# New places in the engines' queues for a fused attention and mixture-of-experts block

## The chip, the cores and the metric
The kernel runs on one core of one Trainium2 chip. The metric is the device time of one execution in microseconds (us). Before the change three runs took 1023.67, 1023.90 and 1024.99 us; the median is 1023.9. All arithmetic is float32. PE is the matmul engine (TensorE), DVE is VectorE, ACT is ScalarE, POOL is GpSimd and SP is SyncE, which here only issues DMAs.

## The reference, cut to what matters
```
xn  = layernorm(x)                                  # x: 4 x 1024 tokens x 128
# attention: 16 query heads, 8 key/value heads of 64, rotary embedding, gate per head
q, k, v, gate = split(xn @ w_attn);  q, k = rope(q), rope(k)
G   = cumsum(log_sigmoid(6.9 + gate))               # over time
a   = exp(2 log|q k / 8| + G_t - G_s - max),  causal
y   = layernorm_per_head(a @ v / (sum(a) + 1e-6)) * ln_w
attn = y @ w_proj
# experts: 7 routed (top 2, capacity 366) and one shared
h   = layernorm(xn) * ln_g + ln_b
idx, gates = top2 softmax(h @ Wr);  pos = place of the token in its expert
routed = gates * ((silu(xe @ W1) * (xe @ W3)) @ W2)  # scattered to the experts and back
shared = (silu(h @ W1s) * (h @ W3s)) @ W2s
out = x + attn + routed + shared
```

## The kernel before
The 4096 tokens are four chunks (the batch rows) of 1024, each eight blocks of 128. The kernel has a setup and then 32 pairs (p = 0 to 31: chunk p // 8, key/value head p % 8, and its two query heads).

**Setup.** For each chunk b, `norms(b)` (L1016) on DVE makes both layer norms in 18 pieces: statistics, two reciprocal roots by Newton steps, and the normalised x. POOL's `normalise` makes the second norm of chunks 1 to 3. On PE `xt` and `ht` transpose the two norms (ACT copies them out), `gate` and `rt` are the products for the forget gates and the router. The shared expert runs over groups of 512 tokens; six of the eight groups are done in setup (`NSH` = 6), each as four slices b: `up` (two 512-column products, L614 and L617), `silu` on ACT (L844), `gate` on DVE (L1280), then `down` in two halves (L624) and `add` on DVE (L1285). "up 2.1" is slice 1 of group 2, "down 2.1" the second half of group 2.

`forget()` (L1079) is one chain on DVE: the logarithm of the sigmoid by a series, then, after the cumulative sums on PE (`cs`, L653 and L654), the tables of the decays; its transposed table goes through `hc` on PE and `hs` on ACT to memory. `route()` (L1153) is another: it copies the router's logits out, finds first and second choice as one-hot tables (v_oh is raised at its 13th step), then needs PE's totals (`tt`, L663), which it copies out (L1198), prefix sums over the blocks, PE's counts (`cn`, L666), makes each token's place, and the gates (v_gk, L1264). With the gates POOL may scatter tokens to the experts' buffer: 64 indirect DMAs (`scatter`, L1534), six of them (`EARLY`) in setup.

K and Q of pair 0: PE projects (L571), ACT copies to RAWk or RAWq (L897, L892), DVE multiplies by the cosine (L1349, L1340), SP swaps the halves with four DMAs (L473), POOL multiplies by the sine and adds (`rotate`, L1502 and L1505). The two head halves of K are then copied crosswise by SP (`keys`, L491 and L492). The first score (L778) needs both halves of Q rotated, and the keys. The last two groups of the shared expert are done at the end (`sup`, L731, with L925 on ACT and L1318 on DVE; `sdn`, L738, with L1326).

**What sets the order.** Each engine works through its queue in order. Setup's queues are the tables `PE_FIRST`, `ACT_FIRST`, `DVE_FIRST` and `POOL_FIRST`: a row (kind, at, by, then, na, nb) puts job (a, b) at place at + by * a + then * b, and `spread` (L89) sorts them. The numbers are places in a plan; only the order that results counts. For the pairs the tables `PE_AT`, `ACT_AT`, `DVE_AT`, `POOL_AT` and `SP_AT` give each job's place within pair p, to which `agenda` (L152) adds 200 + 20 p. On PE the places only say to which batch of five score steps a job belongs: `jobs_of` (L179) puts the jobs of a batch behind its scores and ahead of the value products (L811), the transposes (`FLIPS`) first. The semaphore waits belong to the jobs and move with them. `bank_plan` (L185) gives each job a PSUM bank by the order of the queue.

Per pair: `decay` (L882) on ACT makes the decay tables of the four query blocks, `select` (L1524) on POOL cuts them at the diagonal, `scale` (L1361) on DVE multiplies the diagonal scores with them, `square` (L964) and `weigh` (L960) on ACT square, `top` (L1390 to L1397) on DVE runs the maximum, `rows` on SP (L502) collects it, `fold`, `max` reduce it; `vs` (L1516) on POOL scales V; `nt`, `y`, `sum`, `n1`, `ysq`, `var`, `root`, `n2`, `fin`, `wp` divide, normalise and project. An expert is `weights`, `xe`, `up`, `down`, `combine`, at seven of the pairs.

Of the kernel before, what the change touches and what calls it, by code (L numbers as in the profile page):

```python
# [61 lines left out]
ACT_AT = [(31.70, "sup", 0), (31.80, "sup", 1), (31.90, "sup", 2), (32.00, "sup", 3), (43.80, "sup", 4), (43.90, "sup", 5), (44.00, "sup", 6), (44.10, "sup", 7), (12.8, "nt", 0), (27.18, "nt", 1), (-3.54, "decay", 0), (-3.53, "decay", 1), (5.4, "decay", 2),  # L62
          (10.31, "decay", 3), (23.4, "y", 0), (31.69, "y", 1), (54.54, "fin", 0), (55.63, "fin", 1),
          (43.3, "ysq", 0), (8.58, "xe", 0), (21.82, "up", 0), (23.77, "up", 1), (25.18, "up", 2), (44.23, "up", 3),
          (61.99, "down", 0), (-22.23, "k", 0), (-21.67, "k", 1), (-10.3, "q", 0), (-10.17, "q", 1), (-9.65, "v", 0),
          (10.34, "v", 1), (5.99, "square", 0), (6.69, "square", 1), (13.39, "square", 2), (13.44, "square", 3),
          (13.8, "square", 4), (13.89, "square", 5), (7.75, "weigh", 0), (10.73, "weigh", 1), (12.4, "weigh", 2),
          (14.9, "weigh", 3)]
DVE_AT = [(27.00, "sup", 0), (27.10, "sup", 1), (27.20, "sup", 2), (27.30, "sup", 3), (37.90, "sup", 4), (38.00, "sup", 5), (38.10, "sup", 6), (38.20, "sup", 7), (38.60, "sdn", 0), (49.00, "sdn", 1), (23.72, "fold", 0), (27.44, "max", 0), (49.5, "wp", 0), (54.22, "wp", 1), (27.9, "sum", 0),
          (32.03, "var", 0), (34, "root", 0), (34.29, "root", 1), (37.4, "root", 2), (28.36, "up", 4),  # L70
          (33.13, "up", 5), (41.31, "up", 6), (43.43, "up", 7), (-29.32, "k", 0), (-27.97, "k", 1), (-18.98, "q", 0),
          (-16.07, "q", 1), (-1.12, "scale", 0), (-0.78, "scale", 1), (-0.64, "scale", 2), (4.39, "scale", 3),
          (0.13, "top", 0), (4.37, "top", 1), (5.3, "top", 2), (5.41, "top", 3), (8, "top", 4), (8.38, "top", 5),
          (11.39, "top", 6)]
# [1565 lines left out]
```

## Time and profile before
| | us |
|---|---|
| median of three runs | 1023.9 |
| profiled execution | 1027.59 |
| its span, first to last instruction | 1025.5 |
| PE busy | 964.1 (94%) |
| DVE busy | 881.6 (86%) |
| ACT busy | 678.0 (66%) |
| POOL busy | 628.7 (61%) |
| PE waiting for POOL's rotated Q, 131 to 400 us | 11.2, of which 6.4 at the first score and 4.8 later |

All rows are of the profiled execution, with times from its start. The span lies 2.1 us below the execution's own time. An engine that is busy 94% still has gaps; where they lie is told by a view by stage. An engine's idle time costs something only if a chain that ends last goes through it. In a timeline a bracket gives the idle time of the engine just before the instruction, and the line that ended it.

### The profile page before, as it was taken

To read this page: it belongs to the slowest core of one execution; us is meant where nothing else is said; L and a number is where in the kernel's file an instruction comes from. 1 tells how busy PE (TensorE), PEld (TensorE's weight loads), DVE (VectorE), ACT (ScalarE), POOL (GpSimd) and SP (SyncE) were. 2 spreads that over 40 slices of the span, in tenths; PEclk is the share of its full clock that TensorE was granted. 3 is DMA by queue.
4 is the path that set the end of the run, shared out by engine and by line. 5 is a ranking of instruction groups with operands and counts; after the bars stand their busy time and mean duration, and the time that the engine had idled before them with its cause. 6 is when DMAs were issued, how large, how long until landed. Compare 5 with 4: busy or idle time off the path is not lost.

```text
span 1025.5 us, 23347 instructions
## 1 busy us (share of the span) xinstructions
PE 964.1 (94%) x8871; PEld 709.2 (69%) x8871; DVE 881.6 (86%) x1730; ACT 678.0 (66%) x1078; POOL 628.7 (61%) x593
## 2 busy tenths in 40 slices
...
GB/s 268 97 1 47 57 80 135 100 119 89 119 87 103 97 128 90 104 120 126 84 132 119 104 135 118 94 121 132 81 117 127 111 92 132 98 103 102 136 143 21
DMA packets 78767, 109.44 MB, mean 107 GB/s; under 512 B 15901, under 2 KB 47005, under 8 KB 78528
## 3 DMA queue, kind: packets, MB, share of 16 engines
...
## 4 chain that ended last, share of the span: by engine, by line
PE 71%; DVE 15%; POOL 4%; issue 4%; ACT 3%; DMA 1%; SPq 1%; DVEq 0%; POOLq 0%; ACTq 0%
PE PS L778 20%; PE PS L571 19%; PE PS L811 17%; PE PS L566 6%; DVE PS L1397 2%; PE PS L614 2%; DVE PS L1390 2%; PE PS L617 2%; DVE U L1397 2%; PE PS L624 1%; POOL xe_d L1534 1%; POOL U L1502 1%; DVE SM L1422 1%; PE PS L587 1%; DVE PS L1392 1%
## 5 line engine op out<-in xcount | busy, mean ns | idle before, releaser
L778 PE MATMUL PS<-Qt,Kt 64*128 64x256 f32 (+1 forms) x2560 | 281.0, 369 | 21.0 <-POOL Qt L1505 12.8
L778 PEld LDWEIGHTS PS<-Qt,Kt 64*128 64x128 f32 x2560 | 232.0, 190 | 62.3 <-POOL Qt L1505 14.7
L964 ACT ACTIVATE U<-PS 128x1024 f32<-128x1024 f32 x144 | 141.3, 1023 | 70.7 <-PE PS L778 59.4
L1502 POOL TENSOR_TENSOR U<-U,consts 128x512 f32<-128x512 f32 x96 | 127.3, 1326 | 45.6 <-DMA U<-U 45.5
L811 PE MATMUL PS<-U 128*64 128x256 f32 (+1 forms) x1344 | 141.2, 349 | 0.2 <-ACT U L960 0.2
L811 PEld LDWEIGHTS PS<-U 128*64 128x64 f32 x1344 | 94.0, 137 | 40.4 <-issue 6.0
L1524 POOL TENSOR_SCALAR_AFFINE_SELECT U<-U 128x256 f32<-128x256 f32 x128 | 59.9, 545 | 99.7 <-ACT U L882 99.4
L1570 POOL TENSOR_TENSOR U<-U,SM 128x1024 f32<-128x1024 f32 x32 | 71.7, 2241 | 73.5 <-DVE SM L1417 72.7
L1361 DVE SCALAR_TENSOR_TENSOR U<-PS,U 128x768 f32<-128x768 f32 x96 | 88.6, 953 | 30.8 <-PE PS L778 29.0
L1397 DVE SCALAR_TENSOR_TENSOR PS<-U,ES,PS 128x512 f32<-128x512 f32 x144 | 108.3, 752 | 4.7
L882 ACT ACTIVATE U<-U,negG 128x256 f32<-128x256 f32 (+1 forms) x256 | 98.7, 454 | 9.0 <-DMA U<-H_d 8.2
L1574 POOL TENSOR_TENSOR U<-U,SM 128x1024 f32<-128x1024 f32 x32 | 61.8, 1932 | 60.9 <-DVE SM L1440 60.8
L571 PE MATMUL PS<-XT,W 128*64 128x512 f32 x384 | 94.1, 603 | 0.0
L960 ACT ACTIVATE U<-U 128x768 f32<-128x768 f32 x96 | 81.2, 847 | 16.9 <-DVE U L1361 16.9
L1505 POOL TENSOR_TENSOR Qt<-Qt,U 128x512 f32<-128x512 f32 x64 | 83.6, 1307 | 9.2
L1534 POOL DMA_INDIRECT xe_d<-U,idx_s x64 | 70.1, 1096 | 21.7 <-issue 12.4
L566 PE MATMUL PS<-consts,U 128*128 128x128 f32 x533 | 78.5, 281 | 5.2 <-DVE U L1361 4.1
L566 PEld LDWEIGHTS PS<-consts,U 128*128 128x128 f32 x533 | 58.9, 142 | 20.9 <-issue 11.4
L892 ACT ACTIVATE U<-PS 128x512 f32<-128x512 f32 x64 | 38.1, 597 | 47.7 <-PE PS L571 47.7
L811 PE MATMUL PS<-U,VS 128*64 128x256 f32 x576 | 68.8, 379 | 0.1
L985 ACT ACTIVATE U<-U 128x1008 f32<-128x1008 f32 x32 | 33.4, 1043 | 49.3 <-PE PS L571 25.3
L571 PE MATMUL PS<-Wp,U 128*64 128x128 f32 x1024 | 58.9, 273 | 4.9 <-ACT U L918 4.9
...
## 6 DMA issues: line engine op xcount, KB each, us to landing
G<-U SPq DMA_DIRECT2D x512, 64.0 KB
...
```

The costliest lines, as they stand in the source:

```text
L566: return te.transpose(to, src, ident)
L571: mm = te.matmul(to[lo:lo + 64], weights[:, lo:lo + 64], moving, start=start, stop=stop)
L778: mm = te.matmul(bank[:, 256 * n:256 * n + 256 - lo], Kt[u % 2][(ki + hd) % 2][rows, 128 * j:128 * j + 128], Qt[p % 2][m // 2][rows, 256 * ...
L811: mm = te.matmul(P[4][64 * hd:64 * hd + 64, c + lo:c + 256], vt, A[s % NA][:, o:o + 256 - lo], start=begins and n == 0, stop=ends and n == 1)
L882: ex = s.activation(D[un % 3][:, lo:hi], HR[:, 256 * m + 128 * k2:256 * m + 256], ACT.Exp, scale=0.5, bias=negG[:, n:n + 1])
L960: s.activation(a_, a_, ACT.Square).then_inc(a_sd, 1)
L964: s.activation(A[n % NA], PS[:, first:first + 1024], ACT.Square, scale=0.125, bias=GUARD).then_inc(a_so, 1)
L1361: v.scalar_tensor_tensor(A[s % NA].rearrange("p (a t) -> p a t", a=2)[:, :, 0:384], PS[:, first:first + 1024].rearrange("p (a t) -> p a t" ...
L1397: v.scalar_tensor_tensor(run if i == m and n == 1 else PRUN, a_[:, :, n], es, PRUN, ALU.mult, ALU.max).then_inc(v_mx, 1)
L1502: g.tensor_tensor(sw, sw, sinT[:, cols], ALU.mult).then_inc(made, 1)
L1505: g.tensor_tensor(to, to, sw, ALU.add).then_inc(added, 1)
L1534: g.indirect_dma_start(xe_d[:, :], bass.IndirectOffsetOnAxis(ap=idx_s[:, c:c + 1], axis=0), hn_v[:, k], None, bounds_check=NE * SLOT - 1, ...
```

## The change
Only the tables of places are changed. No instruction, tile, semaphore wait or loop is. `PE_FIRST` and the like are given in full, old and new:

```diff
-PE_FIRST = [("xt", 22, 28.59, 4.36, 4, 2), ("gate", 31.08, 28, 0.97, 4, 2), ("ht", 32.16, 28.14, 5.08, 4, 2),
-            ("rt", 41.4, 27.8, 1.12, 4, 2), ("up", 33.04, 24.16, 6.2, NSH, 4), ("down", 66.9, 24.8, 6.12, NSH, 2),
-            ("wv", 134.1, 0, 0, 1, 1), ("wpe", 138.72, 1, 0, 2, 1), ("cs", 132.53, 0, 0, 1, 1),
-            ("hc", 144.93, 0, 0, 1, 1), ("tt", 155.59, 0, 0, 1, 1), ("cn", 162.68, 0, 0, 1, 1),
-            ("k", 147.14, 4.08, 0, 2, 1), ("q", 167.45, 4, 0, 2, 1), ("v", 159.28, 4.43, 0, 2, 1)]
+PE_FIRST = [('xt', 21.04, 20.01, 3.86, 4, 2), ('gate', 30.85, 18.83, 0.98, 4, 2), ('ht', 32.16, 19.7, 6.55, 4, 2),
+            ('rt', 41.4, 19.46, 1.12, 4, 2), ('up', 34.75, 24.16, 6.21, 6, 4), ('down', 71.01, 25.0, 8.07, 6, 2),
+            ('wv', 124.05, 0, 0, 1, 1), ('wpe', 137.19, 0.46, 0.14, 2, 1), ('cs', 104.38, 0, 0, 1, 1),
+            ('hc', 129.51, 0, 0, 1, 1), ('tt', 131.63, 0, 0, 1, 1), ('cn', 136.22, 0, 0, 1, 1),
+            ('k', 149.2, 4.08, 0, 2, 1), ('q', 178.53, 3.52, 0.72, 2, 1), ('v', 159.29, 2.04, 0, 2, 1)]
-ACT_FIRST = [("xt", 22.31, 28.84, 4.68, 4, 2), ("ht", 37.33, 28.36, 3.36, 4, 2), ("silu", 39.95, 23.79, 6.11, NSH, 4),
-             ("wv", 130.05, 0, 0, 1, 1), ("wp", 143.43, 1.04, 0, 2, 1), ("ex", 117.57, 0, 0, 1, 1),
-             ("hs", 149.37, 0, 0, 1, 1), ("es", 169, 0, 0, 1, 1), ("e1", 172.32, 0, 0, 1, 1),
-             ("k", 151.74, 4.33, 0, 2, 1), ("q", 190.18, 4, 0, 2, 1), ("v", 163.14, 3.92, 0, 2, 1)]
+ACT_FIRST = [('xt', 23.67, 20.16, 6.54, 4, 2), ('ht', 37.33, 20.37, 3.73, 4, 2), ('silu', 39.76, 23.79, 6.11, 6, 4),
+             ('wv', 124.5, 0, 0, 1, 1), ('wp', 136.84, 1.14, 1.09, 2, 1), ('ex', 94.5, 0, 0, 1, 1),
+             ('hs', 127.99, 0, 0, 1, 1), ('es', 132.33, 0, 0, 1, 1), ('e1', 149.32, 0, 0, 1, 1),
+             ('k', 148.91, 4.33, 0, 2, 1), ('q', 211.31, 7.08, 1.25, 2, 1), ('v', 164.69, 3.92, 0, 2, 1)]
-DVE_FIRST = [("norm", 4.77, 29.15, 0.82, 4, 30), ("gate", 39.97, 24.16, 6.28, NSH, 4), ("add", 83.46, 24.04, 0, NSH, 1),
-             ("hl", 110.14, 0, 0, 1, 1), ("one", 132.74, 0, 0, 1, 1), ("forget", 117.51, 0.77, 0, 44, 1),
-             ("logits", 128.9, 0, 0, 1, 1), ("route", 149.17, 0.64, 0, 52, 1), ("k", 153.48, 3.98, 0, 2, 1),
-             ("q", 187.97, 4.31, 0, 2, 1)]
+DVE_FIRST = [('norm', 4.01, 20.4, 0.66, 4, 30), ('gate', 41.02, 24.16, 6.28, 6, 4), ('add', 83.04, 24.13, 0, 6, 1),
+             ('hl', 79.04, 0, 0, 1, 1), ('one', 112.99, 0, 0, 1, 1), ('forget', 94.48, 0.77, 0, 44, 1),
+             ('logits', 103.38, 0, 0, 1, 1), ('route', 129.61, 0.64, 1.29, 52, 1), ('k', 149.03, 3.5, 0, 2, 1),
+             ('q', 169.61, 4.31, 2.09, 2, 1)]
-POOL_FIRST = [("norm", 38.88, 32.76, 0, 3, 1), ("scatter", 170.28, 4.09, 0, EARLY, 1),
-              ("select", 294.1, 6.18, 0, 2, 1), ("vs", 278.5, 0, 0, 1, 1), ("k", 159.29, 8.22, 0, 2, 1),
-              ("q", 232.63, 8.35, 0, 2, 1)]
+POOL_FIRST = [('norm', 0.75, 23.04, 5.64, 3, 1), ('scatter', 117.77, 3.04, 0.31, 6, 1),
+              ('select', 248.17, 7.05, 3.38, 2, 1), ('vs', 278.17, 0, 0, 1, 1), ('k', 149.49, 10.25, 0, 2, 1),
+              ('q', 238.7, 6.58, 0.06, 2, 1)]
```

The orders that come out of them, from where they matter (b: before, a: after; a star gives a count):

```
PE   b: ... up 3.3, rt 3.0, rt 3.1, up 4.0, cs, wv, up 4.1, wpe, wpe, down 3.0, up 4.2, hc, K 0, down 3.1, up 4.3, K 1,
        up 5.0, tt, V 0, up 5.1, cn, V 1, down 4.0, up 5.2, Q 0, Q 1, down 4.1, up 5.3, down 5.0, down 5.1
     a: ... rt 3.0, rt 3.1, up 2.3, down 1.1, cs, up 3.0, up 3.1, up 3.2, down 2.0, wv, up 3.3, down 2.1, hc, up 4.0,
        tt, cn, wpe, up 4.1, wpe, up 4.2, down 3.0, K 0, up 4.3, K 1, down 3.1, up 5.0, V 0, V 1, up 5.1, up 5.2,
        down 4.0, up 5.3, Q 0, down 4.1, Q 1, down 5.0, down 5.1
ACT  b: ... silu 4.3, K 1, silu 5.0, V 0, silu 5.1, V 1, es, silu 5.2, e1, silu 5.3, Q 0, Q 1
     a: ... silu 3.2, wv, hs, silu 3.3, es, silu 4.0, wp, wp, silu 4.1, silu 4.2, K 0, e1, K 1, silu 4.3, silu 5.0, V 0,
        silu 5.1, V 1, silu 5.2, silu 5.3, Q 0, Q 1
DVE  b: norm 0 *30, norm 1 *8, gate 0.0, norm 1 *8, gate 0.1, ... gate 4.2, route, forget, route, forget, route *4, K 0,
        route *3, gate 4.3, route, add 3, route *2, K 1, route *6, gate 5.0, route *9, gate 5.1, route *10, gate 5.2,
        route *10, gate 5.3, add 4, route *4, Q 0, Q 1, add 5
     a: norm 0 *30, norm 1 *26, gate 0.0, norm 1 *4, norm 2 *4, gate 0.1, norm 2 *10, gate 0.2, ... gate 3.2, forget *2,
        route *3, add 2, route *2, gate 3.3, route *8, gate 4.0, route *10, gate 4.1, route *8, K 0, route *2, gate 4.2,
        route *3, K 1, ... add 3, gate 4.3, gate 5.0, gate 5.1, Q 0, Q 1, gate 5.2, add 4, gate 5.3, add 5
POOL b: norm *3, K 0, K 1, scatter *6, Q 0, Q 1, vs, select, select
     a: norm *3, scatter *6, K 0, K 1, Q 0, Q 1, select, select, vs
```

Of the 147 places in the five tables of the pairs 117 are the same or moved by at most 1.0; of the others, old and new place:

```diff
 PE_AT   sup 7: 25.2 -> 26.66, sup 8: 40.8 -> 33.21, sup 14: 41.4 -> 42.83, sup 15: 41.5 -> 54.33,
         fin 1: 58.3 -> 59.37, wp 0: 59.31 -> 57.94, xe: 1.41 -> 0.15, up 5: 36.29 -> 37.4, up 7: 42.31 -> 43.73,
         down: 54.32 -> 50.37
 ACT_AT  sup 4: 43.8 -> 42.3, decay 3: 10.31 -> 11.47, up 0: 21.82 -> 17.69
 DVE_AT  sup 4: 37.9 -> 36.53, sdn 1: 49.0 -> 40.49
 POOL_AT combine 0: 51.94 -> 53.25, combine 1: 66.52 -> 62.5, select 3: 1.22 -> 0.1, vs 1: -16.1 -> -6.3,
         n2: 38.34 -> 37.25, q 0: -15.66 -> -13.54
 SP_AT   sload: 2.0 -> 6.58, rows: -1.59, 8.46, 9.68, 11.17 -> 0.47, 4.46, 7.9, 12.55, swapq: -25.73 -> -27.04,
         row: -14.53 -> -16.28, weights: -10.6, 4.79 -> -7.61, 2.81
...
```

In the pairs this changes PE's order only where an expert's `down` meets two K projections (three times: down first now) and in the last chunk. There it was sup 8 to 15, sdn 0, fin 0, fin 1, sdn 1, wp 0, wp 1 and becomes sup 8 to 13, sdn 0, sup 14, fin 0, fin 1, sup 15, wp 0, sdn 1, wp 1. On POOL vs.1 of a pair moves behind the second Q rotation (`q` 1) of the same pair. On SP keys go behind the third group of rows. On ACT decay 3 goes behind the square of the second diagonal (`weigh` 1); on DVE `sup` 4 goes ahead of the last root step of pair 31.

## Rows read from the trace of the kernel before

**Rows 1.** Stage, us, then PE, PEld, DVE, ACT, POOL busy, granted clock, DMA.
```profile
120.00:140.00 20.00, 13.64 (x82) 11.14 (x83) 4.77 (x7) 6.95 (x11) 12.97 (x15) 0.74 0.29 77
...
200.00:225.00 25.00, 22.08 (x208) 16.21 (x204) 24.10 (x40) 17.76 (x30) 23.01 (x21) 1.00 0.43 108
...
400.00:600.00 200.00, 199.96 (x1954) 146.79 (x1953) 181.15 (x320) 155.28 (x246) 129.25 (x118) 1.00 0.44 112
```

**Rows 2.** Timeline at the end of setup.
```profile
110.21 1.94 PE L571 MATMUL PS<-XT,W 128*64 128x512 f32 x8
...
118.26 1.08 ACT L892 ACTIVATE U<-PS 128x512 f32<-128x512 f32 x2
...
118.61 1.18 POOL L1534 DMA_INDIRECT xe_d<-U,idx_s  x1 [8.97 <-DVE gk L1264]
...
119.37 2.41 SPq L473 DMA_DIRECT2D U<-U  x4
...
126.19 1.30 POOL L1502 TENSOR_TENSOR U<-U,consts 128x512 f32<-128x512 f32 x1
...
130.26 1.26 POOL L1505 TENSOR_TENSOR Qt<-Qt,U 128x512 f32<-128x512 f32 x1
...
131.58 4.64 PE L778 MATMUL PS<-Qt,Kt 64*128 64x256 f32 x20 [6.36 <-POOL Qt L1505]
```

**Rows 3.** Timeline, the next swap and its rotation.
```profile
140.81 2.45 SPq L473 DMA_DIRECT2D U<-U  x4
...
145.31 1.28 POOL L1502 TENSOR_TENSOR U<-U,consts 128x512 f32<-128x512 f32 x1 [0.63 <-DMA U<-U]
```

**Rows 4.** Chain of waits: start, us, engine and line.
```profile
39.87 0.86 PE PS L617 x2
...
46.35 1.89 PE PS L624 x16
```

**Rows 5.** Timeline, PE's waits in setup (PEld: weight loads).
```profile
109.16 1.12 PE L617 MATMUL PS<-U 128*128 128x512 f32 x2 [0.54 <-DVE U L1280]
...
82.88 0.37 PEld L653 LDWEIGHTS PS<-U,consts 128*128 128x128 f32 x2 [0.49 <-DVE U L1113]
```

**Rows 6.** Timeline, DVE's choice steps and copy of the totals.
```profile
93.80 0.39 DVE L1178 TENSOR_REDUCE SM<-U 128x32 f32<-128x224 f32 x1
...
98.78 0.38 DVE L1181 TENSOR_TENSOR U<-consts,SM 128x224 f32<-128x224 f32 x1
...
101.00 0.69 DVE L1198 COPY U<-PS 128x512 f32<-128x512 f32 x1 [1.23 <-PE PS L663]
```

**Rows 7.** Timeline, PE behind long waits and without one.
```profile
119.75 5.47 PE L624 MATMUL PS<-U 128*128 128x128 f32 x32 [2.66 <-DVE acc L1285]
...
180.50 5.64 PE L778 MATMUL PS<-Qt,Kt 64*128 64x256 f32 x40 [2.72 <-POOL Qt L1505]
...
192.43 4.38 PE L778 MATMUL PS<-Qt,Kt 64*128 64x256 f32 x40
```

**Rows 8.** Busy time and granted clock behind two waits.
```profile
119.70:122.00 2.30, 2.25 (x12) 2.25 (x13) 1.18 (x2) 0.00 (x0) 1.70 (x3) 0.59 0.63 152
...
1006.00:1012.00 6.00, 4.45 (x29) 3.25 (x28) 3.86 (x12) 0.60 (x1) 1.90 (x1) 1.00 0.00 1
```

**Rows 9.** Timeline of POOL: K rotations, a mask.
```profile
103.33 1.27 POOL L1502 TENSOR_TENSOR U<-U,consts 128x512 f32<-128x512 f32 x1 [33.57 <-DMA U<-U]
...
108.10 1.53 POOL L1505 TENSOR_TENSOR Kt<-Kt,U 128x512 f32<-128x512 f32 x1
...
190.01 0.50 POOL L1524 TENSOR_SCALAR_AFFINE_SELECT U<-U 128x256 f32<-128x256 f32 x1 [0.95 <-ACT U L882]
```

**Rows 10.** Timeline of the tail.
```profile
1000.36 6.36 PE L731 MATMUL PS<-U 128*128 128x512 f32 x14
...
1008.27 1.12 PE L731 MATMUL PS<-U 128*128 128x512 f32 x2 [1.55 <-DVE Kt L1318]
...
1021.11 0.69 DVE L1313 TENSOR_TENSOR acc<-PS,acc 128x512 f32<-128x512 f32 x1 [1.05 <-PE PS L571]
```

More of the change, by code:

```diff
@@ L62 @@
[L62 to L74, printed above, removed]
@@ new lines @@
+ACT_FIRST = [('xt', 23.67, 20.16, 6.54, 4, 2), ('ht', 37.33, 20.37, 3.73, 4, 2), ('silu', 39.76, 23.79, 6.11, 6, 4), ('wv', 124.5, 0, 0, 1, 1), ('wp', 136.84, 1.14, 1.09, 2, 1), ('ex', 94.5, 0, 0, 1, 1), ('hs', 127.99, 0, 0, 1, 1), ('es', 132.33, 0, 0, 1, 1), ('e1', 149.32, 0, 0, 1, 1), ('k', 148.91, 4.33, 0, 2, 1), ('q', 211.31, 7.08, 1.25, 2, 1), ('v', 164.69, 3.92, 0, 2, 1)]
+DVE_FIRST = [('norm', 4.01, 20.4, 0.66, 4, 30), ('gate', 41.02, 24.16, 6.28, 6, 4), ('add', 83.04, 24.13, 0, 6, 1), ('hl', 79.04, 0, 0, 1, 1), ('one', 112.99, 0, 0, 1, 1), ('forget', 94.48, 0.77, 0, 44, 1), ('logits', 103.38, 0, 0, 1, 1), ('route', 129.61, 0.64, 1.29, 52, 1), ('k', 149.03, 3.5, 0, 2, 1), ('q', 169.61, 4.31, 2.09, 2, 1)]
@@ new lines @@
+POOL_FIRST = [('norm', 0.75, 23.04, 5.64, 3, 1), ('scatter', 117.77, 3.04, 0.31, 6, 1), ('select', 248.17, 7.05, 3.38, 2, 1), ('vs', 278.17, 0, 0, 1, 1), ('k', 149.49, 10.25, 0, 2, 1), ('q', 238.7, 6.58, 0.06, 2, 1)]
+PE_AT = [(24.57, 'sup', 0), (24.6, 'sup', 1), (24.7, 'sup', 2), (24.8, 'sup', 3), (24.9, 'sup', 4), (25.0, 'sup', 5), (25.1, 'sup', 6), (26.66, 'sup', 7), (33.21, 'sup', 8), (40.9, 'sup', 9), (41.0, 'sup', 10), (41.1, 'sup', 11), (41.2, 'sup', 12), (41.47, 'sup', 13), (42.83, 'sup', 14), (54.33, 'sup', 15), (41.5, 'sdn', 0), (58.9, 'sdn', 1), (34.28, 'max', 0), (19.9, 'y', 0), (24.69, 'y', 1), (52.27, 'fin', 0), (59.37, 'fin', 1), (57.94, 'wp', 0), (59.72, 'wp', 1), (0.15, 'xe', 0), (10.81, 'up', 0), (14.9, 'up', 1), (15.75, 'up', 2), (31.73, 'up', 3), (34.72, 'up', 4), (37.4, 'up', 5), (42.01, 'up', 6), (43.73, 'up', 7), (50.37, 'down', 0), (-27.24, 'k', 0), (-27.14, 'k', 1), (-19.3, 'q', 0), (-12.17, 'q', 1), (-11.98, 'v', 0), (9.76, 'v', 1)]
@@ new lines @@
+ACT_AT = [(31.7, 'sup', 0), (31.8, 'sup', 1), (31.9, 'sup', 2), (32.0, 'sup', 3), (42.3, 'sup', 4), (43.9, 'sup', 5), (44.0, 'sup', 6), (44.1, 'sup', 7), (12.82, 'nt', 0), (27.64, 'nt', 1), (-3.54, 'decay', 0), (-3.53, 'decay', 1), (5.5, 'decay', 2), (11.47, 'decay', 3), (23.4, 'y', 0), (31.69, 'y', 1), (54.54, 'fin', 0), (55.63, 'fin', 1), (43.3, 'ysq', 0), (9.08, 'xe', 0), (17.69, 'up', 0), (23.77, 'up', 1), (25.18, 'up', 2), (43.94, 'up', 3), (61.0, 'down', 0), (-22.94, 'k', 0), (-20.85, 'k', 1), (-10.3, 'q', 0), (-10.17, 'q', 1), (-9.65, 'v', 0), (10.31, 'v', 1), (5.74, 'square', 0), (6.97, 'square', 1), (13.39, 'square', 2), (13.44, 'square', 3), (13.8, 'square', 4), (13.89, 'square', 5), (7.78, 'weigh', 0), (10.73, 'weigh', 1), (13.04, 'weigh', 2), (15.23, 'weigh', 3)]
```

11 lines of the change are left out of this document (4 added, 7 removed), and 3 rows, old and new, of the table PE_AT.

## The prediction

> **What bounds the kernel now.** I read the page's busy shares, then busy time by stage, then the timeline at the end of setup and in the tail. PE is busy 199.96 of 200 us between 400 and 600, but 13.6 of 20 between 120 and 140 [rows 1]. In the middle the order of the queues is worth next to nothing unless it makes PE wait; time can come from two places, the setup until the first score at 131.58, and the tail.
>
> The end of setup reads like this [rows 2]: PE has both Q projections at 112.15, ACT copies them only from 118.26 (they stand in its queue behind the last silus and the exponential of the gates), SP issues the half-swap from 119.37, POOL issues six scatters from 118.61 to 126.19 and only then rotates Q, until 131.52; the first score starts at 131.58. Two chains end there close together: gates, scatters, rotation; and copy, swap, rotation. A swap issued at 140.81 let POOL start at 145.31, 4.5 us later [rows 3], so without the scatters the rotation could have begun at 119.37 + 4.5 = 123.9 instead of 126.2.
>
> **The change, part by part.** No instruction is added or removed; every cost is that of a place in a queue.
>
> *Setup on PE.* Work is conserved, so I count from the old run. An up pair costs 0.86 + 0.86 us, 0.1 more behind small matmuls: 1.8; eight down products (half a down) 1.9 [rows 4]. In the new order the last Q projection stands behind one up pair (group 5, slice 3) and one down half (the second of group 4) that came after it before. The old end of Q, 112.15, less the 0.54 us that PE stood in an up ahead of it [rows 5], plus 1.8 + 1.9, is 115.3 if there is no new wait.
>
> New waits: (a) the cumulative sum (cs) stands for the forget chain, 0.5 us before [rows 5]. I write up 2.1 for slice 1 of group 2, and down 2.1 for the second half of group 2. Counting the 16 steps from the exponential behind silu 2.1, PE gets there 1.0 us early: +0.5. (b) The totals (tt) need the one-hot choice, v_oh. In DVE's new queue add 2, which waits for the end of down 2.1 on PE, stands ahead of nine of the choice's steps. Before, these ran from 93.80 to 99.16, 5.4 us with three other operations (a K product, a gate, an add: 1.8) between them: 3.6 [rows 6]. With add 2 (0.6), gate 3.3 (0.6) and two semaphore hops (0.2), v_oh comes 5.0 us after PE ends down 2.1. PE has the H transposes (0.4) and up 4.0 (1.8) in between and stands 2.8 us. (c) The counts (cn) now follow tt directly and need DVE's copy of it, 0.69 [rows 6] and a hop: 0.8; before, a V product and an up pair stood there. The sum is 4.1: Q ends at 119.4.
>
> (d) The clock. PE's wait of 2.66 us before 119.75 was followed by a granted clock of 0.59, and after one of 2.72 us forty score matmuls took 5.64 us instead of 4.38; the 1.55 us before 1008.27 left the clock at 1.00 [rows 7, 8]. The slow stretches cost 1.3 us (scores) and 5.47 - 2 x 1.9 = 1.7 (downs). The new wait of 2.8 us is of the first kind: +1.5, so Q ends at 120.9. Bounds: 0 and 1.7.
> The Trainium skill ("TensorE: Matmul & The Clock Gate", Part 1) has the same mechanism, half clock for an idle array and full clock after sustained work, but counts the ramp as under 1% of a typical span and not worth fitting. By that sentence the 1.5 would be dropped, and the total below would be -3.3 instead of -1.8; the rows show 1.3 to 1.7 for each such wait, so I keep it.
>
> *Setup on ACT, SP, DVE and POOL.* ACT copies the second Q half right behind PE (0.7 with its hop): 121.6, against 119.37 before. The six us that this copy stood in ACT's queue are gone, but what is late next is PE, which brings Q nine us later. With 4.5 for swap and landing POOL can start at 126.1; keys still follow the swap on SP, behind it as before. Is POOL free by then? The first scatter came 17.6 us after DVE began to copy the totals at 101.00 [rows 2, 6]. PE's new down 2.1 ends near 84.5 by the same counting, the copy begins near 92, the first scatter at 109.6 even if nothing in between is faster; six scatters 7.6, both K rotations 6.3 (103.33 to 109.63 [rows 9]): 123.5. So the scatters, which set the start before, are off the path with 2.6 us to spare, and the 8 us or more that they gain, nobody collects. From 126.1 the four operations take 5.4 as before: first score at 131.5 against 131.58. **Setup -0.1 us.** DVE now takes both Q products before gates 5.2 and 5.3 and add 4, so PE stands some 2.8 us ahead of down 5 and ends it near 128: hidden under swap and rotation, with 3.5 us to spare, and its cost is what exceeds that. The decays wait for it and are ready about 131, before the third score, which is the first to need one.
>
> *Between 131 and 985.* On POOL vs.1 goes behind both Q rotations of its pair; its readers are the next pair's first value products, behind a whole block of scores. On SP keys go behind one more group of row copies (four issues, 2.4 us), half a pair before the scores that read them. On ACT decay.3 goes behind one square (0.85), on POOL select.3 ahead of a scatter; on PE an expert's down passes two K projections three times, with its inputs long there. All are hidden by a PE that is full. Value 0; bounds -1.5 and rival C.
>
> *Tail.* The last chunk's order on PE was sup 8 to 15, sdn 0, fin, fin, sdn 1, wp, wp; the last sup stood 1.55 us for DVE [rows 10]. Now sdn 0, whose inputs come from sup 0 to 7, stands before sup 14 and 15. From 1000.36: sup 8 to 13 5.2, sdn 0 3.6, sup 14 0.9: 1010.1. The fins wait for POOL's second scaling, which one moved multiply on DVE makes 0.6 later, 1010.2; fins and sup 15: 1012.0; half wp, sdn 1, half wp 1.8 + 3.6 + 1.8: 1019.3; DVE's add: 1020.1 against 1021.8. **Tail -1.7 us**; bounds 0 and -2.5.
>
> **Sum.** -0.1 - 1.7 = -1.8 us. The profiled execution took 1027.6 (span 1025.5) and becomes 1025.8. The median of the runs shown is 1023.9, 3.7 lower; the difference carries over: **1022.1 us**.
>
> **Rivals.**
> *A, the clock stays up.* If the wait at tt comes out shorter, the 1.5 us go: 1020.6. For: 2.8 is only 0.1 above a wait that cost. Against: both known waits above 2.6 cost.
> *B, the choice is early enough.* If v_oh is there when PE gets to tt, Q comes 3.6 + 1.5 us sooner and the swap chain ends at 126.4; the POOL chain by its bound at 123.5 + 5.4 = 128.9. Time 1022.1 less 2.6 to 5.1: 1017 to 1019.5. For: norms and forget chain do end 10 us earlier. Against: add 2 waits for PE whatever DVE does.
> *C, POOL pays in the early pairs (slower).* Until the 64 scatters are out POOL is busy 23 of 25 us [rows 1]. There select.3 waited 0.95 us for ACT's decay at 190.01 [rows 9]. Now it stands ahead of a scatter and its decay comes 0.85 later: POOL may stand up to 1.3 more in a pair, and Q's rotation, which scores need, is queued behind. If four of the eight early pairs have no slack there, 4 x 1.3 = 5.2: 1027.3. It decides where POOL's stand exceeds what it waits for DVE's sums anyway.
> *D, the tail gives nothing.* If sdn 0 has to wait for its bank, or for sup 4's silu, -1.7 goes: 1023.8.
>
> **Chances.** The forecast 0.38 (1020.5 to 1023.5), A 0.18, B 0.12, C 0.14, D 0.18. About 2 us (0.2%) is what a measurement of this kernel tells from no change: faster is under 1021.9, slower over 1025.9. Faster: A, B and a third of the forecast's own spread, 0.43. Slower: C and a little of D, 0.16. Same: 0.41. The range leaves out the far half of B and of C: 1018 to 1026.5.
>
> **What would show it.** PE's wait at L663 (tt) of 2.5 to 3 us between 84 and 92, with a clock under 0.8 behind it; DVE's third L1285 waiting for L624; the Q copies on ACT (L892) ending at 121 to 122 with no wait behind silu; POOL's first scatter by 109.6 and its Q rotation starting on a DMA, not behind a scatter; first L778 at 130 to 132; no wait above 0.5 at the last L731. It is wrong if the first score starts before 129 or after 133, if PE's waits for POOL's Q between 140 and 350 exceed the 4.8 us of before by more than 1, or if the tail keeps its length.

## The result, and the profile after

The change makes the kernel slower. Four runs took 1032.87 to 1036.89 us, median 1034.4; the kernel before, timed beside it, 1024.4. The ratio is 1.0099, 95% interval 1.0073 to 1.0125, so about 10 us. The forecast was 1022.1, with a range up to 1026.5.

The profiled execution of after is the fastest of its four, 1032.87 us (span 1030.8); before's took 1027.59 (span 1025.5), 3 us above its median. The two traces thus show 5.3 us of the 10. The line numbers of after are those of before less 30: the score is L748, tt L633, the Q rotation L1475.

The stages of after follow, with columns as in [rows 1]. Of the 20 us between 80 and 100 PE was busy 16.3, at a granted clock of 0.83; in this stage the kernel before had neither an idle PE nor a low clock (20.00 busy, 1.00).

```profile
80.00:100.00 20.00, 16.32 (x52) 6.75 (x51) 13.13 (x31) 6.49 (x11) 0.00 (x0) 0.83 0.10 34
100.00:120.00 20.00, 20.00 (x114) 11.62 (x114) 9.20 (x23) 9.12 (x15) 9.49 (x9) 1.00 0.18 47
120.00:140.00 20.00, 15.45 (x100) 12.49 (x98) 6.02 (x9) 7.21 (x12) 9.82 (x12) 0.83 0.23 56
```

Timeline of after, PE around tt: start, duration, and in brackets the wait before it.

```profile
89.18 1.12 PE L633 MATMUL PS<-U,consts 128*128 128x512 f32 x2 [2.89 <-DVE U L1151]
91.09 1.59 PE L636 MATMUL PS<-U,consts 128*128 128x512 f32 x2 [0.78 <-DVE U L1168]
92.61 1.97 PE L617 MATMUL PS<-U,SM 64*64 64x512 f32 x4
94.51 2.07 PE L584 MATMUL PS<-U 128*128 128x512 f32 x2
96.38 1.92 PE L587 MATMUL PS<-U 128*128 128x512 f32 x2
98.22 1.17 PE L617 MATMUL PS<-U,SM 64*64 64x512 f32 x4
```

Both waits are as forecast (2.8 and 0.8). What follows is not. From within cn (L636) on PE is slow, and from 92.6 to 98.2, under the first half of wpe (L617) and up 4.1, the granted clock is 0.50, the lower of its two levels (1.2 GHz). Each half of wpe, with up 4.1 between them, takes a slot of its own.

The end of setup in after, to be laid beside [rows 2]:

```profile
108.84 1.18 POOL L1504 DMA_INDIRECT xe_d<-U,idx_s  x1 [55.83 <-DVE gk L1234]
122.67 1.08 PE L541 MATMUL PS<-XT,W 128*64 128x512 f32 x4
123.80 0.60 ACT L862 ACTIVATE U<-PS 128x512 f32<-128x512 f32 x1 [2.39 <-PE PS L541]
126.36 6.78 PE L594 MATMUL PS<-U 128*128 128x128 f32 x32 [2.62 <-DVE acc L1255]
128.66 1.26 POOL L1472 TENSOR_TENSOR U<-U,consts 128x512 f32<-128x512 f32 x1 [6.88 <-DMA U<-U]
133.30 1.28 ACT L852 ACT_TABLE_LOAD   x1 [8.90 <-PE PS L594]
134.02 2.65 PE L748 MATMUL PS<-Qt,Kt 64*128 64x256 f32 x24 [0.87 <-POOL Qt L1475]
137.74 1.83 PE L748 MATMUL PS<-Qt,Kt 64*128 64x256 f32 x16 [1.07 <-ACT U L934]
```

The rotation now starts on the swap (6.88 for a DMA) and not behind scatters, as forecast, but 2.6 us late, with PE's Q. The last down (L594) took 6.78 us at a granted clock of 0.55; ACT's decays wait for it, and the scores stopped once more for ACT (1.07).

The wait of 2.62 us ahead of this down came in other kernels too, and what followed differed: the same 32 matmuls took 6.78 us here, 5.18 (clock 0.73) in setup_only below and 3.84 (clock 1.00) in after_tt_later. In these rows a wait of this length doesn't by itself tell what it costs.

In the pairs, the start of POOL's first scaling (n1) is a good mark: there is one per pair. After less before, in us: pairs 0 to 2 +2.5; pair 3 +5.4; pair 7 +7.1; pair 18 +3.9; pair 31 +6.6. The timeline of after has these stands (waits of an engine) there:

```profile
143.58 0.40 POOL L1494 TENSOR_SCALAR_AFFINE_SELECT U<-U 128x256 f32<-128x256 f32 x1 [4.43 <-ACT U L852]
...
182.63 6.19 PE L748 MATMUL PS<-Qt,Kt 64*128 64x256 f32 x40 [4.83 <-POOL Qt L1475]
...
235.28 0.79 DVE L1433 COPY U<-gk 128x32 f32<-128x32 f32 x1 [1.08 <-DMA xe_d<-U,idx_s]
...
241.33 2.23 PE L748 MATMUL PS<-Qt,Kt 64*128 64x256 f32 x24 [1.85 <-DVE acc L1283]
...
249.03 0.88 POOL L1494 TENSOR_SCALAR_AFFINE_SELECT U<-U 128x256 f32<-128x256 f32 x1 [3.47 <-ACT U L852]
```

L1494 is rival C's stand, POOL waiting for ACT's decays: 22.4 us between 131 and 400 in all, 12.3 in before. L1433 is the copy of the gates, which waits for 32 landed scatters. L1283 is new: the scores' bank is still held by the projection (wp 1), which DVE has not yet added; it happens three times (1.85, 1.25, 1.07). PE's waits for POOL's rotated Q between 140 and 350 are 8.3 us, 4.9 in before. The tail, to be laid beside [rows 10], takes from the last n1 to PE's end 18.6 us instead of 19.9.

```profile
1006.70 5.32 PE L701 MATMUL PS<-U 128*128 128x512 f32 x12
1011.85 3.73 PE L708 MATMUL PS<-U 128*128 128x128 f32 x32
1015.42 1.02 PE L701 MATMUL PS<-U 128*128 128x512 f32 x2
...
1024.39 1.97 PE L541 MATMUL PS<-Wp,U 128*64 128x128 f32 x32
```

### The profile page after: what moved, and what is told of

Read it like the earlier page. It is cut to its first block, busy times and chain, and to the rows that moved or that the text cites. A ratio compares the mean times of both kernels' runs of the same rounds, so it can differ in the third digit from the quotient of the medians.

```text
span 1030.8 us, 23346 instructions
## 1 busy us (share of the span) xinstructions
PE 967.4 (94%) x8871; PEld 706.2 (69%) x8871; DVE 879.6 (85%) x1730; ACT 679.1 (66%) x1078; POOL 621.5 (60%) x593
## 4 chain that ended last, share of the span: by engine, by line
PE 68%; DVE 17%; POOL 6%; issue 5%; DMA 2%; ACT 1%; SPq 1%; POOLq 0%; DVEq 0%; ACTq 0%
PE PS L748 18%; PE PS L541 18%; PE PS L781 16%; PE PS L536 6%; DVE PS L1367 3%; PE PS L584 2%; PE PS L594 2%; DVE PS L1360 2%; PE PS L587 2%; DVE U L1367 2%; POOL xe_d L1504 2%; POOL U L1472 1%; DVE SM L1392 1%; DVE PS L1362 1%; PE PS L557 1%
## 5 line engine op out<-in xcount | busy, mean ns | idle before, releaser
L748 PE MATMUL PS<-Qt,Kt 64*128 64x256 f32 (+1 forms) x2560 | 279.9, 368 | 21.0 <-POOL Qt L1475 11.4
L748 PEld LDWEIGHTS PS<-Qt,Kt 64*128 64x128 f32 x2560 | 228.4, 189 | 64.9 <-POOL Qt L1475 13.2
L1494 POOL TENSOR_SCALAR_AFFINE_SELECT U<-U 128x256 f32<-128x256 f32 x128 | 64.6, 582 | 140.3 <-ACT U L852 140.1
L1472 POOL TENSOR_TENSOR U<-U,consts 128x512 f32<-128x512 f32 x96 | 131.2, 1366 | 10.9 <-DMA U<-U 10.5
L1475 POOL TENSOR_TENSOR Qt<-Qt,U 128x512 f32<-128x512 f32 x64 | 85.4, 1335 | 9.2
L955 ACT ACTIVATE U<-U 128x1008 f32<-128x1008 f32 x32 | 33.5, 1046 | 54.0 <-PE PS L541 27.8
```

Source lines behind the costliest of these rows:

```text
L748: mm = te.matmul(bank[:, 256 * n:256 * n + 256 - lo], Kt[u % 2][(ki + hd) % 2][rows, 128 * j:128 * j + 128], Qt[p % 2][m // 2][rows, 256 * ...
L1472: g.tensor_tensor(sw, sw, sinT[:, cols], ALU.mult).then_inc(made, 1)
L1475: g.tensor_tensor(to, to, sw, ALU.add).then_inc(added, 1)
```

## The experiments

All are edits of the tables of places. Each kernel was timed in five rounds beside the kernel before (median then 1024.3 to 1025.9), so ratios, with 95% intervals, are what to compare. Where tables are written on one line, line numbers are lower: the score L778 is L760 in pairs_only and pairs_rot_back, L763 in pairs_pool_back, L766 in setup_only and fixed_setup_mixed.

**Which part?**

```diff
 setup_only:         the four *_FIRST tables new, the rest old
 pairs_only:         the *_AT and SP_AT tables new, the rest old
 after_select_back:  (after) ACT decay 3: 11.47 -> 10.31; POOL select 3: 0.1 -> 1.22
 after_add_later:    (after) DVE_FIRST add: by 24.13 -> 27.5
```

> The kernel before with the four new setup tables alone; the tables of the pairs, the tail's among them, are the old ones. Theory 1 (the late setup is carried and grows): first score at 134.0 as in the kernel after, and the DVE copy L1463 that waits for 32 landed scatters stands about 1 us in pair 3, so that the +2.5 us become +5 there; time 1029.5 to 1031.5 against 1024.4 before, since the old tail gives nothing. Theory 2 (the pairs' new places on POOL and ACT make the loss): +2.5 us from the first score on and no more, 1027.

Measured: 1027.6 us, ratio 1.0018 (1.0004 to 1.0032). First score at 134.58, but at full clock: the forty scores took 4.12 us where those of before took 6.69, so at pair 0 it was only 0.4 us behind. Before first, then setup_only:

```profile
131.58 6.69 PE L778 MATMUL PS<-Qt,Kt 64*128 64x256 f32 x40 [6.36 <-POOL Qt L1505]
```

```profile
134.58 4.12 PE L766 MATMUL PS<-Qt,Kt 64*128 64x256 f32 x40 [2.47 <-POOL Qt L1493]
```

The late start is neither carried nor grown: by n1 it is 0.2 us behind in pair 31.

> The kernel before with the new tables of the pairs alone (tail included), setup as before. Theory 1: first score at 131.6, no growth in the early pairs, tail -1.3: 1023. Theory 2: POOL's cut of the fourth decay table (select 3, L1524) stands 2 to 4 us for ACT in several early pairs as in the kernel after, PE waits longer for the rotated Q, and the time is 1026 to 1030 in spite of the tail.

Measured: 1031.1, 1.0057 (1.0040 to 1.0073). The larger part of the loss is in the pairs, the part that the forecast set to 0.

> The kernel after with two places back: decay 3 on ACT at 10.31 and select 3 on POOL at 1.22. Theory 2: POOL's waits for ACT's decay between 131 and 400 us fall from 22 to about 12 us, and the time falls from 1034.4 by 3 to 5 us. Theory 1: the waits fall the same way, but what is queued behind them had slack, and the time stays within 1 us of 1034.4.

Measured: 1038.9, 1.0123 (1.0102 to 1.0143), no faster than after. POOL's waits for the decays fell from 22.4 to 10.5 us, as expected, and the time did not fall with them: rival C's mechanism is there and is not what makes after slow. The median is even 4.5 us above after's, though the intervals overlap; by n1 its trace falls behind after's from pair 15 on, by 2.4 us there and 7.6 in pair 30, and why stays open.

> The kernel after with the shared expert's adds on DVE spread wider (83.04 + 27.5 per group instead of 24.13), so that add 2 stands behind the choice's steps. Theory 1: PE's wait at the totals (L633, tt) falls from 2.9 us to under 1.5 and the clock behind it stays up; Q's last projection ends 3 to 6 us earlier and the first score comes at 130 to 131.5, bound by POOL's scatters; the time falls by 3 us, by 5 if the jump in pair 3 goes as well. Theory 2: first score the same, but only those 3 us.

Measured: 1031.3, 1.0058 (1.0037 to 1.0079), about 4 us better than after, yet not for the reason given: the wait at tt was still 2.70 us, since a gate product, which waits for ACT's silu, stands ahead of the choice too (DVE idle 3.33 us there). My arithmetic of the stand was right and its cause incomplete. In its trace the first forty scores end 2.0 us sooner than in after; where the rest comes from stays open.

**What in the pairs?**

```diff
 before_tail:      (before) PE sup 7, 8, 13, 14, 15, ACT sup 4, DVE sup 4, sdn 0, sdn 1: new places
 pairs_rot_back:   (pairs_only) POOL k 1: -15.04 -> -15.9; q 0: -13.54 -> -15.66
 before_rot_late:  (before) POOL k 1: -15.9 -> -15.04; q 0: -15.66 -> -13.54
 pairs_wp_early:   (pairs_only) DVE wp 1: 54.28 -> 51.5
```

> The kernel before with the tail's new places alone (sup 7, 8, 13, 14, 15 on PE, sup 4 on ACT, sup 4, sdn 0 and sdn 1 on DVE). The prediction's term: the stretch from POOL's last first scaling to PE's last instruction is 18.6 us as in the kernel after instead of 19.9, the time 1.3 to 1.7 us under before. Rival: the gain belongs to the lateness of the kernel after, and the time is that of before within 0.5.

Measured: 1025.2, 0.9986 (0.9974 to 0.9999): the tail is worth 1.4 us by the ratio, between nothing and 2.7.

> The kernel before with the two rotation places of the change alone (k 1 at -15.04, q 0 at -13.54 on POOL). Theory 3: the waits of PE's scores for the acc add (L1313) appear between 230 and 350 us, and the time is 2 to 4 us over before. Theory 2b: no such wait, within 1 us of before.

Measured: 1030.9, 1.0049 (1.0036 to 1.0063). Two places alone cost 5.0 us. The bank wait came only once (1.10 us at 293.17); PE stood longer for rotated Q as well: behind the first score 7.6 us up to 400, 4.8 in before.

> The new tables of the pairs with two places of POOL back: the second K rotation at -15.9 and the first Q rotation at -15.66, ahead of a scatter again. Theory 3 (phase): behind the scatter the Q rotation runs beside DVE's first running maximum of the next block (L1372 in the kernel pairs_only, 0.70 us alone and 1.71 beside it), and POOL's scatters beside DVE's small steps of the roots, so that DVE adds the projection (wp 1) 1 to 2 us later against PE and PE's second scores of the batch wait 1.1 to 1.9 us for its bank in three early pairs (4.2 us in all). Here these waits go, and the time falls by 3 to 4 us against pairs_only: 1027 to 1028 where pairs_only had 1031.1 and before 1025.9. Theory 2b (select 3 and the keys are to blame, not the rotation): the waits stay, 1031.

Measured: 1029.4, 1.0047 (1.0028 to 1.0065), not told apart from pairs_only. In its trace the bank wait shrank to 0.5 us, as theory 3 has it, but 3.0 us were still lost between the n1 of pairs 2 and 3; putting two places back among the other new ones doesn't undo what they cost alone. The traces of before_select_early and before_gates_early below lose 1.8 and 1.2 us at the same point, and neither kernel is slower at the end; what makes the 3.0, and why they stay, is open.

> The new tables of the pairs with one DVE job moved: the add of the second half of the projection (wp 1) ahead of the variance steps (51.5 instead of 54.28). If the wait of PE's scores for that add's bank is what makes the early pairs late, it is gone whatever makes DVE late: no wait for the acc add between 131 and 400 us, and the time is 3 to 4 us under pairs_only's 1031.1. If the bank wait only hides another one behind it (POOL's Q rotation, DVE's K product), PE waits there instead and the time stays within 1 us of 1031.

Measured: 1032.0, 1.0061 (1.0048 to 1.0074). The bank wait was gone, and in its place PE stood for DVE's product with the decay (1.55 at 240.66, 1.50 at 295.29, 1.54 at 349.59). The bank was a symptom: DVE is late, whatever of it PE meets first.

One thing that makes DVE late shows in two timelines. First pairs_only, where the rotation of Q (POOL L1487) has begun just before DVE's first running maximum (L1372); then pairs_rot_back, in another pair, where a scatter stands there instead:

```profile
281.71 1.27 POOL L1487 TENSOR_TENSOR Qt<-Qt,U 128x512 f32<-128x512 f32 x1
281.82 1.71 DVE L1372 SCALAR_TENSOR_TENSOR PS<-U,ES 128x512 f32<-128x512 f32 x1
```

```profile
224.54 1.00 POOL L1516 DMA_INDIRECT xe_d<-U,idx_s  x1 [0.15 <-issue]
224.63 0.70 DVE L1372 SCALAR_TENSOR_TENSOR PS<-U,ES 128x512 f32<-128x512 f32 x1
```

The same instruction takes 0.70 us beside a scatter and 1.71 beside the rotation: 281.71 + 1.27 = 282.98, then 0.55 more. It waits until POOL has finished. The Trainium skill (SBUF — State Buffer, "Who interferes with whom") states it: a DVE instruction with two SBUF inputs contends with a GpSimd instruction that reads SBUF, and whichever issues second is blocked until the first has ended. L1372 reads two tiles from SBUF, the rotation reads SBUF, and the trace agrees. The maximum of the next steps (L1397 in before), whose second input lies in PSUM, keeps its 0.75 us throughout (mean 753 ns of 47).

The groups of that line between 131 and 400 us (count, then busy us and mean ns), in before, in before_rot_late, and in pairs_only and pairs_rot_back:

```profile
L1390 DVE SCALAR_TENSOR_TENSOR PS<-U,ES 128x512 f32<-128x512 f32 x20 | 20.0, 1001 | 1.7 <-ACT U L960 0.8
L1390 DVE SCALAR_TENSOR_TENSOR PS<-AX,ES 128x512 f32<-128x512 f32 x6 | 7.8, 1298 | 1.0 <-ACT U L964 0.5
```

```profile
L1390 DVE SCALAR_TENSOR_TENSOR PS<-U,ES 128x512 f32<-128x512 f32 x20 | 23.6, 1178 | 2.6 <-DMA G<-U 0.8 <-issue 0.7 <-ACT U L964 0.4
L1390 DVE SCALAR_TENSOR_TENSOR PS<-AX,ES 128x512 f32<-128x512 f32 x6 | 9.0, 1505 | 0.6
```

```profile
L1372 DVE SCALAR_TENSOR_TENSOR PS<-U,ES 128x512 f32<-128x512 f32 x20 | 22.0, 1100 | 1.3 <-issue 0.4
```

```profile
L1372 DVE SCALAR_TENSOR_TENSOR PS<-U,ES 128x512 f32<-128x512 f32 x20 | 16.7, 835 | 1.4 <-DMA G<-U 0.5 <-DVE U L1379 0.2
```

The same 26 instructions cost DVE 27.8 us in before and 32.6 with the two rotations behind a scatter, 4.8 more on an engine busy 244 of these 269 us. How one such meeting reaches PE can be followed in before_rot_late, at the end of pair 0:

```profile
172.24 0.76 DVE L1390 SCALAR_TENSOR_TENSOR PS<-AX,ES 128x512 f32<-128x512 f32 x1
```

```profile
172.59 1.86 DVE L1390 SCALAR_TENSOR_TENSOR PS<-AX,ES 128x512 f32<-128x512 f32 x1
172.62 1.27 POOL L1505 TENSOR_TENSOR Qt<-Qt,U 128x512 f32<-128x512 f32 x1
176.98 2.27 POOL L1570 TENSOR_TENSOR U<-U,SM 128x1024 f32<-128x1024 f32 x1 [1.66 <-DVE SM L1417]
181.96 6.78 PE L778 MATMUL PS<-Qt,Kt 64*128 64x256 f32 x40 [3.83 <-POOL Qt L1505]
```

The first line is before, the others are before_rot_late. The maximum takes 1.1 us longer beside the rotation, POOL's scaling (L1570) waits for DVE and starts 1.45 us later than in before (175.53), the next Q rotation stands behind it, and PE's scores start at 181.96 instead of 180.50 [rows 7]. Behind the longer wait (3.83 against 2.72) they also take 6.78 us instead of 5.64. That makes 2.6 of the 3.5 us by which this trace is longer than before's.

This doesn't carry over to the change as it stands. There the 26 instructions take 29.3 us in pairs_only (22.0 and 7.3) and 29.0 in after, hardly more than the 27.8 of before; with the two places back they take 24.5 (16.7 and 7.8), and the kernel isn't measurably faster. So the meeting is shown as a cause in before_rot_late; how much of the change's own loss comes through it is not shown.

**The rest of the pairs, and the setup.**

```diff
 pairs_pool_back:      (pairs_only) POOL_AT old; ACT decay 3: 11.47 -> 10.31
 before_select_early:  (before) POOL select 3: 1.22 -> 0.1; ACT decay 3: 10.31 -> 11.47
 after_tt_later:       (after) PE_FIRST tt: 131.63 -> 140; cn: 136.22 -> 144.5; wpe: (137.19, 0.46, 0.14) -> (137.0, 0.46, 0)
 fixed_setup_tail:     (before_tail) *_FIRST of after_tt_later, and PE q: (166, 0.5), ACT q: (167, 0.5), v: (164.69, 1.5),
                       DVE q: (170, 0.5), POOL k: (110, 1)
```

> The new tables of the pairs with POOL's whole old table and decay 3 on ACT at its old place; new in it are PE, DVE (the gates copy ahead of top 6), SP and the tail. If the loss of the pairs (1031.1 against 1025.9, and 1029.4 with the rotations alone put back) lies in POOL's order, this is the kernel before with the new tail: 1025, no wait of PE for the acc add before 400 us, no wait over 2 us of POOL for the decay. If SP's order (keys behind one more group of rows) or the gates copy carries it, it stays at 1028 to 1031.

Measured: 1027.6, 1.0025 (1.0011 to 1.0039). POOL's order with decay 3 carries about half of the pairs' loss (1.0057 to 1.0025, some 3.3 us; which of its places, I didn't part); something else is left. Its profiled execution, at 1031.5 us the slowest of twelve, points to one thing: SP issues pair 2's keys behind both groups of rows, and PE waits for them.

```profile
171.32 4.95 SPq L487 DMA_DIRECT2D G<-U  x8
176.32 0.59 SPq L476 DMA_DIRECT2D Kt<-Kt  x1
176.95 0.60 SPq L477 DMA_DIRECT2D Kt<-Kt  x1
```

```profile
181.07 6.79 PE L763 MATMUL PS<-Qt,Kt 64*128 64x256 f32 x40 [4.10 <-DMA Kt<-Kt]
```

> The kernel before with select 3 at 0.1 on POOL and decay 3 at 11.47 on ACT alone: the mechanism of the prediction's rival C, priced there at up to 5.2 us. Rival C: POOL stands 2 to 3.5 us for the fourth decay table in several early pairs, the Q rotations behind come later, and the time is 2 to 5 us over before. Otherwise (rotations alone are to blame): POOL stands the same, PE does not, within 1 us of before.

Measured: 1025.7, 1.0002 (0.9990 to 1.0014). POOL waited for the decays 23.9 us between 131 and 400, 12.3 in before, so the mechanism of rival C is there, and alone it costs nothing that the interval lets one see (at most 1.4 us).

> The kernel after with three places of PE's setup queue changed: totals (tt) behind up 4.1, counts (cn) behind up 4.2, and the two halves of wpe next to each other. The clock term of the prediction (a stand of 2.8 us costs 1.5 us behind it) measured 3.4 in the trace, and the parted halves of wpe 1.0 more. If that is right, PE's waits at tt and cn go (2.9 and 0.8), the granted clock from 80 to 100 us is 1.00, cn, wpe and up 4.1 take their full-speed times, PE's last Q projection ends 7 to 8 us earlier than 123.75 and the first score, bound by Q's swap and rotation, comes at 127 to 129 if POOL's scatters do not hold it; the time falls by as much only if the pairs can use it: 1029 to 1032 against after's 1034.4. If the clock falls anyway, PE gains only the 3.7 us of waits.

Measured: 1028.8, 1.0030 (1.0020 to 1.0040): three places win back 7 of the 10 us. PE's timeline, to be laid beside that of after above:

```profile
86.45 1.09 PE L617 MATMUL PS<-U,SM 64*64 64x512 f32 x8
87.47 1.13 PE L584 MATMUL PS<-U 128*128 128x512 f32 x2
88.43 1.02 PE L587 MATMUL PS<-U 128*128 128x512 f32 x2
89.42 1.12 PE L633 MATMUL PS<-U,consts 128*128 128x512 f32 x2
...
92.10 1.02 PE L636 MATMUL PS<-U,consts 128*128 128x512 f32 x2
92.96 1.95 PE L594 MATMUL PS<-U 128*128 128x128 f32 x16
```

No wait at tt or cn (one of 1.64 us for DVE comes at 98.61), a granted clock of 1.00 from 80 to 100, first score at 127.97, 6.0 us sooner than in after. The starts give wpe 1.02, up 4.1 1.95, tt 0.96 and cn 0.86: 4.8 us of work. In after the same work filled 89.18 to 99.32 less the 0.78 wait, 9.4: behind the stand of 2.9 us another 4.6 us were lost, of which the parting of wpe is about 1 and the low clock about 3.6.

> Made to beat both: the kernel before's tables of the pairs with the new tail (1025.2 alone), the new setup with tt, cn and wpe placed as in after_tt_later, and in addition Q's projections, copies and products ahead of the last two up pairs, and POOL's K rotations ahead of the scatters. PE idles under 2 us in setup and ends the last down at 123 to 125, POOL's Q rotation ends about the same time: first score 124 to 127 against 131.6. If the early pairs carry it, 1019 to 1021; if POOL, busy 23 of 25 us with the scatters there, takes it back, 1023 to 1025.

Measured: 1018.5, 0.9929 (0.9914 to 0.9945): 7 us faster than before, a little under what was expected. The first score, at 127.92, came later than the 124 to 127 expected: PE ended the last down at 122.6 and then stood 5.32 us for the Q rotation, behind six scatters.

**What was still open.**

```diff
 before_sp_new:          (before) SP_AT new
 pairs_pool_sp_back:     (pairs_pool_back) SP_AT old
 before_gates_early:     (before) DVE top 6: 11.39 -> 11.87
 fixed_setup_new_pairs:  (fixed_setup_tail) all *_AT and SP_AT new
 fixed_setup_mixed:      (fixed_setup_tail) POOL_FIRST scatter: (100, 10), k: (125, 1), q: (145, 1)
 fixed_mixed_select:     (fixed_setup_mixed) POOL select 3: 1.22 -> 0.1; ACT decay 3: 10.31 -> 11.47
```

> The kernel before with SP's new table of places alone. In pairs_pool_back PE's scores of pair 2 waited 4.1 us for the keys (both groups of rows stood ahead of them on SP, issued 176.3 instead of 174.6), in the kernel before 2.7 for the Q rotation. Theory 4 (SP's order carries a part of the loss): the wait for the keys shows at pair 2 here too, POOL's first scaling of pair 1 comes 1.5 to 2.5 us later than before, and the time is 1 to 2 us over before. Rival (PE would have stood there for Q anyway, and the pairs behind have the slack): within 0.7 us of before.

Measured: 1027.5, 1.0016 (1.0001 to 1.0032). The time has the sign of theory 4; the trace doesn't show the wait: its keys went out at 172.80, and PE waited for Q. That the keys are near the edge, and only some executions meet it, would fit both, and is not shown.

> pairs_pool_back with SP's old table as well: what is new is PE's order (the experts' down ahead of two K projections, the tail), DVE's gates copy ahead of top 6 in pair 3, and the tail of ACT and DVE. Theory 4: 1024.5 to 1026, the kernel before with the new tail (-0.7). If PE's order at the experts or the gates copy costs, it stays at pairs_pool_back's +2.2: 1027.5.

Measured: 1025.0, 0.9996 (0.9988 to 1.0005), apart from pairs_pool_back (from 1.0011 up). SP's order is the rest of the loss, about 3 us, and PE's new order at the experts shows no cost beyond the noise (before_tail 0.9986).

> The kernel before with DVE's top 6 at 11.87, which puts the gates copy, waiting for 32 landed scatters, ahead of it in pair 3, and changes nothing else. In the traces with it DVE stood 0.6 to 1.1 us there. Theory: DVE's running maximum and all behind it come that much later once; the time is within 1 us of before. Rival: it sets off the wait of PE's scores for wp 1's bank in the early odd pairs, and costs 2 us or more.

Measured: 1026.2, 1.0005 (0.9996 to 1.0014): no measurable cost, at most 1.4 us.

> The setup of fixed_setup_tail with the new tables of the pairs. If what the setup gains and what the pairs lose add up: 1018.5 plus 5 to 6, 1023 to 1025. If the loss in the pairs comes only in one phase of the engines (POOL's against DVE's), the earlier start shifts it, and it can be anything between 1018 and 1026.

Measured: 1027.7, 1.0024 (1.0013 to 1.0036). The new pairs cost 0.57% with the old setup and 0.95% with the mended one: gains and losses don't add.

> fixed_setup_tail (1018.5) with POOL's setup queue mixed: three scatters, the K rotations, two scatters, the Q rotations, the last scatter. In fixed_setup_tail POOL stood for K's swap until 109.4 with its scatters ready from 104.2, and rotated Q only behind all six of them, until 127.9, while PE had ended the last down at 122.6. By the durations of that trace three scatters fill 104.3 to 109.4, Q's rotation runs from 118.4 to 123.8, PE stands 1.2 us instead of 5.3 and keeps its clock: first score at 124 instead of 127.9 and the forty scores 4.1 us instead of 6.8, together up to 6.7 us. If the early pairs, which POOL bounds, carry it: 1012 to 1015; if POOL's sixth scatter and the pairs take it back: 1016 to 1019.

Measured: 1017.1, 0.9928 (0.9909 to 0.9947). First score at 122.87, 5 us sooner than in fixed_setup_tail; the decays, behind the last down and a table load on ACT, then stopped the scores for 2.00 us:

```profile
122.87 2.65 PE L766 MATMUL PS<-Qt,Kt 64*128 64x256 f32 x24
127.53 2.56 PE L766 MATMUL PS<-Qt,Kt 64*128 64x256 f32 x16 [2.00 <-ACT U L952]
```

In its profiled execution (span 1014.7 against 1017.6) 3 us of the 5 arrive; the ratio shows no more than fixed_setup_tail's. Where the runs lose them is open.

> fixed_setup_mixed with select 3 at 0.1 on POOL and decay 3 at 11.47 on ACT, the one part of the change's pairs that cost nothing alone (1025.7 against 1025.3). If POOL's stand for the decay is free here too: within 1 us of fixed_setup_mixed. If the earlier start makes POOL the bound of more pairs: 2 us or more slower.

Measured: 1018.2, 0.9937 (0.9917 to 0.9956). The medians differ by 1.1 us, well within the intervals, so here too the wait for the decay shows no cost of its own; a cost of up to nearly 4 us the intervals can't exclude.

## Why the prediction was wrong

- *New waits of PE in setup.* Right: 0.46, 2.89 and 0.78 at cs, tt and cn against 0.5, 2.8 and 0.8; Q copied at once by ACT; scatters from 108.84, off the path (forecast: at latest 109.6); swap to POOL 4.2 against 4.5.
- *The clock, "+1.5, bounds 0 and 1.7".* Mis-sized. It measured about 3.6, outside its bounds, and with the parting of wpe, which I had left out, 4.6 (PE's two halves of wpe run together when adjacent, 1.09 for eight; apart, a slot of about 1.0 each). Both rows of [rows 7] that gave the 1.5 were of unbroken work behind one wait; here a second wait of 0.78 followed, which may be why, and no run parts the two. Q ended at 123.75, not at 120.9, the first score came at 134.02, not 131.5, outside the 129 to 133 that the prediction allowed itself. after_tt_later removes this together with the two waits that were forecast, and gains 7 us.
- *"down 5 ... hidden, with 3.5 us to spare".* Wrong in after's profiled execution: begun late and at a granted clock of 0.55, it ended at 133.1 against "near 128", and the decays behind it held up the scores (1.07 us).
- *"Between 131 and 985 ... value 0; bounds -1.5 and rival C".* The step that failed most. "All are hidden by a PE that is full" was a reason taken from the stage between 400 and 600 us; in the early pairs PE does wait. pairs_only measures 5.8 us by its ratio, with the tail's gain in it: by the ratios about 3.3 go with POOL's order and decay 3, about 3 with SP's order. The text weighed vs 1, decay 3, select 3, keys and down. It left out q 0, which stands in the list of moves (by 2.12) and by the tables goes behind a scatter in seven of the early pairs, and k 1 (by 0.86, not listed), which does so once. The two cost 5 us alone (before_rot_late). There the trace shows how: POOL's rotation and DVE's maximum meet, a cost inside the duration of DVE's instructions, where I had looked only for waits on semaphores, and Q comes late to PE behind it. Put back among the other new places they gain no more than noise, so through what the 3.3 us of POOL's order come in the change itself stays open. The prediction's own sign came true: PE's waits for POOL's Q between 140 and 350 exceed the 4.8 of before by more than 1 (8.3).
- *Keys, "hidden".* SP's order costs about 3 us by the ratios of pairs_pool_back and pairs_pool_sp_back, and 1.6 alone (before_sp_new). That it is the keys shows in one trace only, a slow one: PE waits 4.10 us for them at pair 2 of pairs_pool_back.
- *Rival C.* Its stand came, larger than priced (3.47 us at 249.03, where POOL had not waited before and up to 1.3 was expected), and alone it cost nothing measurable: before_select_early 1.0002. A stand of POOL isn't a stand of PE.
- *Tail -1.7.* 1.3 in after's trace, 1.4 by the ratio of before_tail, whose interval reaches almost to 0.
- *The sum.* By ratios setup 0.18% and pairs 0.57% make 0.75%, after 0.99% (0.73 to 1.25): within the interval, though the mended setup shows that they interact (0.57% with the old setup, 0.95% with the mended one). How much of the last 2.5 us is that, and how much scatter between executions, stays open.
